# Sixteen batches of attention: the preparation stage moved between the units of the attention rows

## The chip, the cores and the metric

The program runs on one core of a Trainium2 chip, as one launch. The metric is the device time of that launch in microseconds (us). The engines named below are TensorE (PE: matmuls and transposes), VectorE (DVE), ScalarE (ACT), GpSimd (POOL) and SyncE (SP), whose queue issues every DMA of this program.

## The reference, cut to what matters

`x` is 16 batches of 512 positions by 128 features, float32. Attention has 16 heads of 8 features; a relative position, clipped to 20 on either side, adds a term to the scores and one to the output. The second half (a small attention, then a routed feed-forward layer with 9 experts) reads the same normalised input.

```python
xn = _layernorm(x)                                   # per position
q, k, v = proj(Wq, bq), proj(Wk, bk), proj(Wv, bv)   # of xn, 16 heads of 8
attn1 = einsum('bhqd,bhkd->bhqk', q, k)
attn2 = einsum('bhqd,qkd->bhqk', q, rel_k[idx])      # 41 relative places
attn = softmax((attn1 + attn2) / sqrt(8))
w1 = einsum('bhqk,bhkd->bhqd', attn, v)
w2 = einsum('bhqk,qkd->bhqd', attn, rel_v[idx])
x = x + (w1 + w2) @ Wo.T + bo + ffn(xn)
```

## The kernel before, in words

Four stages run one after the other, each with its own buffers and semaphores, and hand batches over through DRAM: `prepare`, `attend`, `mix`, `experts`. Positions stand on the 128 partitions, so a batch is four tiles of 128 by 128.

`prepare` goes over the 16 batches. For each it loads `X`, takes the statistics (L216, L227 on VectorE; L263, L266 on GpSimd), writes the normalised `XN`, transposes it on TensorE (L367) and copies it out as `XNT` (L327). Three projections follow: q (L352), k (L354), v (L357). Queries, keys and keys less the far-left term (`T[0]` to `T[2]`) are each split into three bf16 parts whose sum is the float32 value: a high part (L221, L316), the rest (L232, L273) cast to a middle part (L234, L323), and a low part (L248, L285). `QR` is the product of the queries with the 40 relative keys (L344, read out at L201 and L305). All of it goes to DRAM: `y` (x + bo), `xn`, nine `parts`, `v`, four tiles of `qr`, and `qr0`.

`attend` takes one batch as a row of 16 units. A unit u has four heads for each of the four blocks of 32 positions in a tile of 128 queries; it is worked in two pairs. In a pair, TensorE computes scores into one half of `b_s` (L682), VectorE adds the relative window (L815) and takes the maxima (L846), ScalarE exponentiates (L919), and in the next unit TensorE transposes the result (L694) into one of two PSUM banks, `b_pt`, from which ScalarE (L899) and VectorE (L832) copy it in turn. Three units later TensorE multiplies with v (L715). Everything that passes through the two banks is listed in `JOBS`; the banks alternate along that list, and a job waits until the reader of the job two places ahead is done (`bank_free`). Every fourth unit has "features" (L728, L732) for the relative output, read at L931 and L868, and multiplied in the next unit (L743). GpSimd makes windows (`make_window`), features and the `V` tiles (`make_v`).

Each engine's stream is written out by hand and keeps its order. SyncE issues, per row, windows in units 2, 6, 10 and 14 (`load_win`), features in units 1, 5, 9 and 13, the probabilities of each unit, and the 18 loads of the next row's queries and keys, spread over the units by the table `SPREAD` (`load_qk`, L566). The first scores of a row wait for all 18 (`qk_in`).

## Time and profile before

| | us |
|---|---|
| median of 3 runs | 2536.8 |
| lowest and highest | 2535.61, 2541.07 |
| the profiled execution | 2541.16 |
| its span in the profile | 2539.2 |

| engine | busy us | share of the span |
|---|---|---|
| PE | 2166.0 | 85% |
| DVE | 1971.7 | 78% |
| ACT | 1574.5 | 62% |
| POOL | 995.5 | 39% |

The profiled execution is one more run of the same program; its span is what the rows below add up to. The shares are means over four stages with different limits, so they don't say what bounds a stage. Stage 1 takes the first 234 us, attention 239 to about 1645 us, and the last two stages the rest.

### The profile page before, as it was taken

The page shows a single profiled execution, that of the slowest core. Times are in us where ns is not written, and L with a number is a line of the kernel's source. Part 1 is how long each engine was busy: PE and PEld are TensorE (multiplying, and loading weights), DVE is VectorE, ACT ScalarE, POOL GpSimd, SP SyncE. Part 2 cuts the span into 40 slices and gives each one's busy share as a digit, 9 for nine tenths or more (in the row PEclk, how much of TensorE's full clock was granted, in tenths as well). Part 3 has the DMA queues.
Part 4 walks back from the last instruction along what each step waited for, and adds up shares of the span by engine and source line. Part 5 has one row for each costly group of instructions (what it writes and reads, how often), then busy time and mean ns, then how long its engine had stood idle before and what let it go on. Part 6 is the DMA issues. An engine that isn't in the chain of part 4 may idle for free. (4 is left out here: it accounts for less than half of the span.)

```text
span 2539.2 us, 78048 instructions
## 1 busy us (share of the span) xinstructions
PE 2166.0 (85%) x27816; PEld 1483.5 (58%) x27816; DVE 1971.7 (78%) x4345; ACT 1574.5 (62%) x3954; POOL 995.5 (39%) x1318
## 2 busy tenths in 40 slices
PE   5673488888888888888888888789999996999999
PEld 3442366666666666666666666546666554666665
DVE  5664399898989889888999999646776765787777
ACT  4442378787877777777878787546777662232222
POOL 5664245445554555455545554300000003333332
PEclk9877699999999999999999999879999998999999
DMA  6887255555554555545555554300101011011010
GB/s 192 268 256 224 81 111 123 110 115 111 125 113 110 117 119 113 116 105 124 111 115 118 118 119 88 65 18 26 37 25 37 25 33 60 29 30 32 25 37 17
DMA packets 572137, 241.21 MB, mean 95 GB/s; under 512 B 466374, under 2 KB 535750, under 8 KB 567238
## 3 DMA queue, kind: packets, MB, share of 16 engines
q1 hardware_dynamic: 571846, 237.28, 37.5%
q8 instruction: 189, 3.10, 0.5%
q14 instruction: 102, 0.84, 0.1%
HBM read 133.87 MB, written 103.29 MB: 93 GB/s over the span
## 5 line engine op out<-in xcount | busy, mean ns | idle before, releaser
L919 ACT ACTIVATE a_probs<-a_bank_s,a_neg_max 128x512 f32<-128x512 f32 x1024 | 694.0, 684 | 203.2 <-DVE a_neg_max L846 199.6
L846 DVE TENSOR_REDUCE a_neg_max<-a_bank_s 128x2 f32<-128x1024 f32 x512 | 626.9, 1224 | 55.7 <-DVE a_bank_s L815 1.4
L694 PE MATMUL a_bank_pt<-a_ident,a_probs 128*128 128x128 f32 x4096 | 590.9, 284 | 54.2 <-ACT a_feat_t L931 42.3
L694 PEld LDWEIGHTS a_bank_pt<-a_ident,a_probs 128*128 128x128 f32 x4096 | 443.1, 142 | 193.1 <-issue 68.8
L899 ACT ACTIVATE a_probs_t<-a_bank_pt 128x512 f32<-128x512 f32 x512 | 304.9, 596 | 146.9 <-PE a_bank_pt L694 144.8
L832 DVE COPY a_probs_t<-a_bank_pt 128x512 f32<-128x512 f32 x512 | 349.3, 682 | 27.5 <-PE a_bank_pt L694 22.1
L715 PE MATMUL a_bank_o<-a_probs_t,a_v 128*32 128x128 f32 x8192 | 285.9, 282 | 1.0
L682 PE MATMUL a_bank_s<-a_kl,a_q 48*32 48x204 bf16 (+14 forms) x3840 | 156.2, 273 | 128.7 <-DMA a_kl<-scr_parts 78.9
L1589 ACT ACTIVATE e_gate<-e_bank_g 128x512 f32<-128x512 f32 x144 | 85.9, 597 | 275.8 <-PE e_bank_g L1528 275.8
L715 PEld LDWEIGHTS a_bank_o<-a_probs_t,a_v 128*32 128x32 f32 x8192 | 215.0, 112 | 56.7 <-issue 33.8
L1005 POOL TENSOR_TENSOR a_win<-a_raw,a_band 128x1152 f32<-128x1152 f32 x64 | 168.6, 2634 | 126.8 <-DVE a_neg_max L846 69.6
L815 DVE TENSOR_TENSOR a_bank_s<-a_bank_s,a_win 128x144 f32<-128x144 f32 (+2 forms) x640 | 161.4, 270 | 57.9 <-PE a_bank_s L682 52.7
L1536 PEld LDWEIGHTS e_bank_y<-e_w,e_hid 128*128 128x128 f32 x1152 | 149.5, 192 | 96.6 <-issue 57.0
L1278 DVE TENSOR_REDUCE m_neg_max<-m_bank_s 128x2 f32<-128x1024 f32 x128 | 156.6, 1224 | 61.4 <-PE m_bank_s L1242 54.1
L919 ACT ACTIVATION_READ_ACCUMULATOR a_probs<-a_bank_s,a_neg_max 128x1 f32 x1024 | 203.2, 198 | 0.0
L682 PEld LDWEIGHTS a_bank_s<-a_kl,a_q 48*32 48x32 bf16 x3840 | 63.2, 89 | 219.1 <-issue 203.6
L1375 ACT ACTIVATE m_probs<-m_bank_s,m_neg_max 128x512 f32<-128x512 f32 x256 | 173.3, 682 | 13.4 <-DVE m_neg_max L1278 5.0
L1251 PEld LDWEIGHTS m_bank_pt<-m_ident,m_probs 128*128 128x128 f32 x1024 | 112.5, 143 | 99.7 <-issue 83.4
L1536 PE MATMUL e_bank_y<-e_w,e_hid 128*128 128x128 f32 x1152 | 156.0, 279 | 17.1 <-DVE e_hid L1698 17.1
L682 PE MATMUL a_bank_s<-a_k,a_q 48*32 48x512 bf16 (+15 forms) x4096 | 169.3, 291 | 0.0
L1341 POOL TENSOR_TENSOR m_rms<-m_rms,m_pows 128x4 f32<-128x4 f32 x16 | 16.1, 1007 | 371.3 <-DVE m_rms L1291 371.3
L1613 DVE SCALAR_TENSOR_TENSOR e_y<-e_bank_y,e_comb,e_y 128x128 f32<-128x128 f32 x512 | 143.8, 343 | 12.3
(166 smaller groups left out, 3576.3 us busy)
## 6 DMA issues: line engine op xcount, KB each, us to landing
scr_probs<-a_probs SPq DMA_DIRECT2D x512, 72.0 KB, 2.7
a_raw<-scr_qr SPq DMA_DIRECT2D x256, 96.0 KB
scr_qr<-p_qr SPq DMA_DIRECT2D x64, 320.0 KB, 2.9
a_feat<-scr_probs SPq DMA_DIRECT2D x256, 78.0 KB, 2.4
scr_parts<-p_sp SPq DMA_DIRECT2D x144, 128.0 KB, 2.9
a_left<-scr_probs SPq DMA_DIRECT2D x256, 64.0 KB, 2.4
a_q<-scr_parts SPq DMA_DIRECT2D x32, 192.0 KB
a_k<-scr_parts SPq DMA_DIRECT2D x32, 192.0 KB
```

The costliest lines, as they stand in the source:

```text
L682: ins = nc.tensor.matmul(b_s[g * QBLK:(g + 1) * QBLK, p, a:z], Q[s][par:par + ROWS, half, at:at + QBLK], keys[s][par:par + ROWS, half, a:z ...
L694: ins = nc.tensor.transpose(b_pt[bank_of(job)][:, 0, t * P:(t + 1) * P], probs[(u - 1) % 4][:, j, MAX_REL + t * P:MAX_REL + (t + 1) * P], ...
L715: ins = nc.tensor.matmul(out, V[s][:, V_SLOTS.index((edge, kt)), j, hh * 24:hh * 24 + 32], blocks[:, :, :, kt * P + j * QBLK:kt * P + (j + ...
L815: ins = nc.vector.tensor_tensor(near, near, bass.AP(own.tensor, own.offset, [own.ap[0], [step, n], [1, z - a]]), ALU.add)
L832: nc.vector.tensor_copy(probs_t[(u - 1) // 2 % 2][:, spot(u - 1, PLACES[j]), :], b_pt[bank_of(job)][:, 0, :]).then_inc(pt_ev[bank_of(job)], 1)
L846: nc.vector.tensor_reduce(neg_max[:, 2 * pair:2 * pair + 2], b_s[:, 2 * pair:2 * pair + 2, :], AX.X, ALU.max, negate=True).then_inc(max_ok, 1)
L899: nc.scalar.activation(probs_t[(u - 1) // 2 % 2][:, spot(u - 1, PLACES[j]), :], b_pt[bank_of(job)][:, 0, :], ACT.Copy).then_inc(pt_ev[bank ...
L919: nc.scalar.activation(probs[u % 4][:, j, MAX_REL:MAX_REL + S], b_s[:, j, :], ACT.Exp, bias=neg_max[:, j:j + 1], accum_out=sums[:, t, PLAC ...
L1005: nc.gpsimd.tensor_tensor(win[t % 2][:], over, band[:].rearrange("p (o h c) -> p o h c", o=1, h=1) .to_broadcast([P, NQB, NJ, WIN]), ALU.m ...
L1278: nc.vector.tensor_reduce(neg_max[:, 2 * pair:2 * pair + 2], b_s[:, 2 * pair:2 * pair + 2, :], AX.X, ALU.max, negate=True).then_inc(max_ok, 1)
L1375: nc.scalar.activation(probs[:, j, :], b_s[:, j, :], ACT.Exp, bias=neg_max[:, j:j + 1], accum_out=sums[s][:, u, j:j + 1]).then_inc(exp_ok, 1)
L1536: ins = nc.tensor.matmul(b_y[k][:, t * P:(t + 1) * P], hid[k][:, t * P:(t + 1) * P], w2[:, e, :], start=True, stop=True)
```

## The change

`prepare` is gone; its buffers, now single instead of double, and its work are in `attend`. Row b, while it attends batch b, prepares batch b + 2 (`LEAD`). Twelve new jobs go through the two `b_pt` banks (`PREP`): the transposed input in unit 3, q in 5, k in 6, v in 13, and the relative products, two each in units 10, 11, 14 and 15. Batch 0 is prepared before any row (`prep(-LEAD, u)` on every engine), batch 1 in a row of its own (`lead=True`) beside the first loads. Rows 0 to 13 carry a preparation; rows 14 and 15 carry none.

Part by part:

- VectorE keeps the statistics (unit 0), `T[0]` (unit 5) and half of each relative read-out, to which a small copy into `QR0` is added. The normalising moves to GpSimd, as two passes over the whole tile; so does the rest and the low part of the queries.
- ScalarE makes `T[1]`, now `T[2]` from `T[1]`, all high and middle parts, `XNT`, and v directly into `v_in`: v no longer goes through DRAM.
- `y` is no longer stored. `attend` loads x again and GpSimd adds `bo` (`bo_ok`).
- A relative product contracts 64 rows of `T[0]` instead of 128.
- The 18 query and key loads now stand in units 3 to 14 instead of 0 to 14, since the low parts are stored in unit 1 of the same row and must have landed by unit 3.

```diff
...
 
-def prepare(nc, x, w, scr, ident_dram):
...
+LEAD = 2
 JOBS = [(u, "probs", j) for u in range(UNITS) for j in range(NJ)]
 JOBS += [(u, "features", n) for u in range(0, UNITS, 4) for n in range(2)] + [(9, "out", n) for n in range(2)]
+PREP = [(3, "xt", 0), (5, "q", 0), (6, "k", 0), (13, "v", 0)] + [(u, "qr", n) for u in (10, 11, 14, 15) for n in range(2)]
+JOBS += PREP
...
-        SPREAD = [1, 1, 2, 1, 1, 1, 2, 0, 1, 1, 2, 1, 2, 1, 1, 0]
+        SPREAD = [0, 0, 0, 2, 1, 1, 2, 2, 1, 1, 2, 1, 2, 2, 1, 0]
...
+            row(-1, 1, -1, lead=True)
...
 
-            def row(b, s, m, first=False, tail=False):
+            def prep(b, u):
+
+                n = b + LEAD
+                if n >= B:
+                    return
+                if u == 4:
+                    sp.wait_ge(xn_ok, n + 1)
+                    sp.dma_start(scr["xn"][n], X[:]).then_inc(out_xn, 16)
+                if u == 11:
+                    for k in range(3):
+                        sp.wait_ge(hi_ok[k], n + 1)
+                        sp.dma_start(scr["parts"][n, k, 0], SP[k][0][:]).then_inc(out_sp, 16)
+                if u == 12 and n + 1 < B:
+                    job_done(sp, b, (3, "xt", 0))
+                    sp.wait_ge(out_xn, 16 * n + 16)
+                    load_x(n + 1)
+                if u in (11, 12, 15):
+                    store_qr(b, (11, 12, 15).index(u))
+                if u == 15:
+                    for k in range(3):
+                        sp.wait_ge(mid_ok[k], n + 1)
+                        sp.dma_start(scr["parts"][n, k, 1], SP[k][1][:]).then_inc(out_sp, 16)
+
+            def store_qr(b, t):
+                n, u = b + LEAD, (10, 11, 14, 15)[t]
+                for hf in range(2):
+                    job_read(sp, b, (u, "qr", hf))
+                sp.dma_start(scr["qr"][n * NT + t], QR[t % 2][:].rearrange("p h r -> p (h r)")).then_inc(out_qr, 16)
+
+            def prep_rest(n):
+                store_qr(n - LEAD, NT - 1)
+                for i in range(NQB):
+                    rows_of = QR0[i * QBLK:(i + 1) * QBLK].rearrange("p t (g h) -> p (t g) h", h=NJ)
+                    sp.dma_start(scr["qr0"][n, :, :, i], rows_of).then_inc(out_0, 16)
+                for k in range(3):
+                    sp.wait_ge(lo_ok[k], n + 1)
+                    sp.dma_start(scr["parts"][n, k, 2], SP[k][2][:]).then_inc(out_sp, 16)
+
+            def row(b, s, m, first=False, tail=False, lead=False):
                 last = isinstance(b, int) and b == B - 1
                 for u in range(12 if tail else UNITS):
                     t = u // 4
...
 
                     if not tail and u % 4 == 2 and not (last and t >= NT - 2):
+                        if t == 1 and not last:
+                            sp.wait_ge(out_qr, 16 * NT * (b + 2))
                         load_win(b + (t >= NT - 2), (t + 2) % NT)
                     if u % 4 == 1 and not (first if u == 1 else tail):
                         read_features(b, u)
-                    if not tail and not last and u == 0:
+                    if not tail and not last and u == 1:
+                        prep_rest(b + 1)
+                    if not tail and not last and u == 3:
+                        need(sp, s_ps, b, 2 * UNITS, 0)
...
+            for u in range(UNITS):
+                prep(-LEAD, u)
+            prep_rest(0)
...
+            def prep(b, u):
+                n = b + LEAD
+                if n >= B:
+                    return
+                for job in PREP:
+                    if job[0] != u:
+                        continue
+                    bank = b_pt[bank_of(job)][:, 0]
+                    bank_free(pe, b, job)
+                    if job[1] == "xt":
+                        pe.wait_ge(xn_ok, n + 1)
+                        for t in range(NT):
+                            ins = nc.tensor.transpose(bank[:, t * P:(t + 1) * P], X[:, t, :], ident[:])
+                    elif job[1] in ("q", "k"):
+                        job_read(pe, b, (3, "xt", 0))
+                        ins = nc.tensor.matmul(bank, (wq if job[1] == "q" else wk)[:], XNT[:], start=True, stop=True)
+                    elif job[1] == "v":
+                        for t in range(NT):
+                            ins = nc.tensor.matmul(bank[:, t * P:(t + 1) * P], XNT[:, t * P:(t + 1) * P], wv[:],
+                                                   start=True, stop=True)
+                    else:
+                        job_read(pe, b, (5, "q", 0))
+                        t, hf = (10, 11, 14, 15).index(u), job[2]
+                        rows_of = slice(hf * HALF, hf * HALF + HALF)
+                        ins = nc.tensor.matmul(bank[:, 0:G * FAR], T[0][rows_of, t * P:(t + 1) * P],
+                                               relx[rows_of, hf::2, :], start=True, stop=True)
+                    ins.then_inc(pt_ps, 1)
 
             def scores(b, u, pair, s):
...
-
+                    prep(b, u)
+
+            for u in range(UNITS):
...
+            def read_qr(b, u, t):
+                n, job = b + LEAD, (u, "qr", 0)
+                bank = b_pt[bank_of(job)][:, 0, 0:G * FAR].rearrange("p (h r) -> p h r", r=FAR)
+                job_done(v, b, job)
+                need(v, out_qr, n, 16 * NT, 16 * 2 * (t // 2))
+                need(v, out_0, n, 16 * NQB, 0)
+                nc.vector.tensor_copy(QR0[:, t, 0::2], bank[:, :, 0])
+                nc.vector.tensor_copy(QR[t % 2][:, 0::2, :], bank).then_inc(pt_ev[bank_of(job)], 1)
+
+            def prep(b, u):
+                n = b + LEAD
+                if n >= B:
+                    return
+                if u == 0:
+                    v.wait_ge(x_in, 16 * n + 16)
+                    need(v, xn_ok, n, 1, 0)
+                    for t in range(NT):
+                        ins = nc.vector.bn_stats(stats[:, t, :], X[:, t, :])
+                    ins.then_inc(stats_ok, 1)
+                    v.wait_ge(stats_ok, n + 1)
+                    for t in range(NT):
+                        ins = nc.vector.bn_aggr(mv[:, t, :], stats[:, t, :])
+                    ins.then_inc(mv_ok, 1)
+                if u == 5:
+                    job = (5, "q", 0)
+                    job_done(v, b, job)
+                    need(v, rest_ok[0], n, 1, 0)
+                    v.wait_ge(prep_ok, 3)
+                    nc.vector.tensor_scalar(T[0][:], b_pt[bank_of(job)][:, 0, :], Q_SCALE, bias_q[:], ALU.mult, ALU.add
...
+            def read_qr(b, u, t):
+                n, job = b + LEAD, (u, "qr", 1)
+                bank = b_pt[bank_of(job)][:, 0, 0:G * FAR].rearrange("p (h r) -> p h r", r=FAR)
+                job_done(act, b, job)
+                need(act, out_qr, n, 16 * NT, 16 * 2 * (t // 2))
+                need(act, out_0, n, 16 * NQB, 0)
+                nc.scalar.activation(QR0[:, t, 1::2], bank[:, :, 0], ACT.Copy)
+                nc.scalar.activation(QR[t % 2][:, 1::2, :], bank, ACT.Copy).then_inc(pt_ev[bank_of(job)], 1)
+
+            def high(n, k):
+                need(act, out_sp, n, PART_STORES, 0)
+                nc.scalar.activation(SP[k][0][:], T[k][:], ACT.Copy).then_inc(hi_ok[k], 1)
+
+            def middle(n, k):
+                act.wait_ge(rest_ok[k], n + 1)
+                nc.scalar.activation(SP[k][1][:], rest[k][:], ACT.Copy).then_inc(mid_ok[k], 1)
+
+            def prep(b, u):
+                n = b + LEAD
+                if n >= B:
+                    return
...
+                    job = (3, "xt", 0)
+                    job_done(act, b, job)
+                    nc.scalar.activation(XNT[:], b_pt[bank_of(job)][:, 0, :], ACT.Copy).then_inc(pt_ev[bank_of(job)], 1)
...
+                    job = (6, "k", 0)
+                    job_done(act, b, job)
+                    need(act, lo_ok[1], n, 1, 0)
+                    nc.scalar.activation(T[1][:], b_pt[bank_of(job)][:, 0, :], ACT.Identity, bias=qk_bias[:, 1:2]
+                                         ).then_inc(pt_ev[bank_of(job)], 1)
+                    job_read(act, b, (5, "q", 0))
+                    high(n, 0)
+                if u == 7:
+                    job_read(act, b, (6, "k", 0))
+                    high(n, 1)
+                    need(act, lo_ok[2], n, 1, 0)
+                    nc.scalar.activation(T[2][:], T[1][:], ACT.Identity, bias=left_less[:]).then_inc(t2_ok, 1)
+                if u == 9:
+                    act.wait_ge(t2_ok, n + 1)
+                    high(n, 2)
+                if u in (10, 11, 14, 15):
+                    read_qr(b, u, (10, 11, 14, 15).index(u))
+                if u in (12, 13, 14):
+                    middle(n, u - 12)
...
+                        act.wait_ge(const_ok, N_CONST_OK - 1)
+                    nc.scalar.activation(v_in[:], b_pt[bank_of(job)][:, 0, :].rearrange("p (t e) -> p t e", e=E), ACT.Copy
+                                         ).then_inc(pt_ev[bank_of(job)], 1)
+
...
+            def prep(b, step):
+                n = b + LEAD
+                if n >= B:
+                    return
+                if step == 0:
+                    g.wait_ge(mv_ok, n + 1)
+                    nc.gpsimd.tensor_tensor(rstd[:], mv[:, :, 1], pows[:, 0:1].to_broadcast([P, NT]), ALU.add
+                                            ).then_inc(rstd_add, 1)
+                    g.wait_ge(rstd_add, n + 1)
+                    nc.gpsimd.tensor_tensor(rstd[:], rstd[:], pows[:, 1:2].to_broadcast([P, NT]), ALU.pow).then_inc(rstd_ok, 1)
+                    nc.gpsimd.tensor_tensor(X[:], X[:], mv[:, :, 0:1].to_broadcast([P, NT, E]), ALU.subtract
+                                            ).then_inc(x_less, 1)
+                    g.wait_ge(rstd_ok, n + 1)
+                    g.wait_ge(x_less, n + 1)
+                    nc.gpsimd.tensor_tensor(X[:], X[:], rstd[:].rearrange("p (t o) -> p t o", o=1).to_broadcast([P, NT, E]),
+                                            ALU.mult).then_inc(xn_ok, 1)
+                if step == 2:
+                    g.wait_ge(t2_ok, n + 1)
+                    for k in range(3):
+                        g.wait_ge(hi_ok[k], n + 1)
+                        need(g, lo_ok[k], n, 1, 0)
+                        nc.gpsimd.tensor_tensor(rest[k][:], T[k][:], SP[k][0][:], ALU.subtract).then_inc(rest_ok[k], 1)
+                if step == 3:
+                    need(g, out_sp, n, PART_STORES, 0)
+                    for k in range(3):
+                        g.wait_ge(mid_ok[k], n + 1)
+                        nc.gpsimd.tensor_tensor(SP[k][2][:], rest[k][:], SP[k][1][:], ALU.subtract).then_inc(lo_ok[k], 1)
+
...
                         scale(b)
+                    if t == 0:
+                        prep(b, 0)
...
-                        make_v(b + 1, t, 1 - s)
+                    if not last and t < 2:
+                        for kt in (2 * t, 2 * t + 1):
+                            make_v(b + 1, kt, 1 - s)
                     if t == 2 and not first:
                         add_out(b)
+                    if t > 1:
+                        prep(b, t)
 
             def scale(b):
...
-    prepare(nc, a["x"], a, scr, a["ident"])
...
```

TensorE at the end of unit 10 and the start of unit 11 of a row, before. L715 is the product with v, L694 the transposes of the probabilities, L682 the scores:

```order
L715 MATMUL a_bank_o<-a_probs_t,a_v 32x128 x16
L694 MATMUL a_bank_pt<-a_ident,a_probs 128x128 x8
L682 MATMUL a_bank_s<-a_kl,a_q 32x236 x4
L682 MATMUL a_bank_s<-a_kl,a_q 32x300 x4
L682 MATMUL a_bank_s<-a_k,a_q 32x276 x4
L682 MATMUL a_bank_s<-a_k,a_q 32x212 x4
L694 MATMUL a_bank_pt<-a_ident,a_probs 128x128 x8
```

The same place now (L500, L479 and L467 are the same operations):

```order
L500 MATMUL a_bank_o<-a_probs_t,a_v 32x128 x16
L479 MATMUL a_bank_pt<-a_ident,a_probs 128x128 x8
L449 MATMUL a_bank_pt<-a_relx,a_t 128x320 x2
L467 MATMUL a_bank_s<-a_kl,a_q 32x236 x4
L467 MATMUL a_bank_s<-a_kl,a_q 32x300 x4
L467 MATMUL a_bank_s<-a_k,a_q 32x276 x4
L467 MATMUL a_bank_s<-a_k,a_q 32x212 x4
L479 MATMUL a_bank_pt<-a_ident,a_probs 128x128 x8
```

Two products of 320 columns stand between the last transposes of a unit and the scores of the next.

VectorE at the end of unit 11, before. L846 is the maxima, L832 the copy of a transposed tile, L825 sums of moved probabilities, L815 the window of unit 12:

```order
L846 TENSOR_REDUCE a_neg_max<-a_bank_s 128x2
L832 COPY a_probs_t<-a_bank_pt 128x512
L825 TENSOR_REDUCE a_moved<-a_probs 128x2 x4
L815 TENSOR_TENSOR a_bank_s<-a_bank_s,a_win 128x2x72
L846 TENSOR_REDUCE a_neg_max<-a_bank_s 128x2
```

The same place now (L688, L670, L663 and L653 are the same operations, L597 and L598 read the relative product out):

```order
L688 TENSOR_REDUCE a_neg_max<-a_bank_s 128x2
L670 COPY a_probs_t<-a_bank_pt 128x512
L663 TENSOR_REDUCE a_moved<-a_probs 128x2 x4
L597 COPY a_qr_first<-a_bank_pt 128x8
L598 COPY a_qr<-a_bank_pt 128x8x40
L653 TENSOR_TENSOR a_bank_s<-a_bank_s,a_win 128x2x72
L688 TENSOR_REDUCE a_neg_max<-a_bank_s 128x2
```

The two copies out of the relative product stand behind the sums and ahead of the next window.

SyncE in units 11 to 13, before. L566 loads keys, L632 stores the output, L643 stores probabilities, L600 and L606 load features:

```order
L643 DMA scr_probs<-a_probs 128x2x72 x2
L566 DMA a_kl<-scr_parts 16x1x4096
L632 DMA scr_y<-a_y_in 128x512
L643 DMA scr_probs<-a_probs 128x2x72 x2
L566 DMA a_kl<-scr_parts 8x4096
L566 DMA a_kl<-scr_parts 24x1x4096
L643 DMA scr_probs<-a_probs 128x2x72 x2
L600 DMA a_left<-scr_probs 32x16x32 x4
```

Now (L272 loads keys, L323 stores high parts, L339 a relative tile, L250 loads the x of a later batch, L391 stores probabilities, L302 loads features):

```order
L391 DMA scr_probs<-a_probs 128x2x72 x2
L323 DMA scr_parts<-a_sp 128x512 x3
L339 DMA scr_qr<-a_qr 128x640
L272 DMA a_kl<-scr_parts 24x1x4096
L380 DMA scr_y<-a_y_in 128x512
L391 DMA scr_probs<-a_probs 128x2x72 x2
L250 DMA a_x<-in_x 128x4x128
L339 DMA scr_qr<-a_qr 128x640
L272 DMA a_kl<-scr_parts 16x1x4096
L272 DMA a_kl<-scr_parts 8x4096
L391 DMA scr_probs<-a_probs 128x2x72 x2
L302 DMA a_left<-scr_probs 32x16x32 x4
```

Six DMAs of the preparation stand in these two units, ahead of the key loads of units 11 and 12.

## Rows read from the trace of the kernel before

**Rows 1.** Windows of the trace: us, each engine's busy us, TensorE's clock, DMA share, GB/s.

```profile
10.00:234.00 224.00, 147.32 (x512) 95.26 (x512) 142.44 (x336) 102.23 (x193) 144.48 (x224) 0.85 0.83 252
234.00:284.30 50.30, 0.00 (x0) 0.00 (x0) 4.74 (x14) 0.00 (x0) 6.68 (x5) 0.50 0.29 86
384.20:1630.20 1246.00, 1089.45 (x19844) 799.86 (x19844) 1117.94 (x2259) 975.70 (x2463) 619.10 (x911) 0.98 0.50 113
```

**Rows 2.** Timeline, first batch in stage 1: start, us, engine, line, tiles, count.

```profile
9.91 0.86 DVE L216 BATCH_NORM_STATS2 p_stats<-p_x 128x6 f32<-128x128 f32 x4
...
32.58 2.79 SPq L169 DMA_DIRECT2D scr_qr<-p_qr  x4
```

**Rows 3.** Timeline, start of the attention stage.

```profile
243.49 2.59 SPq L574 DMA_DIRECT2D a_left_of<-scr_qr  x4
...
248.53 4.00 SPq L566 DMA_DIRECT2D a_q<-scr_parts  x6
...
284.35 0.23 PE L682 MATMUL a_bank_s<-a_kl,a_q 48*32 48x44 bf16 x4 [60.70 <-DMA a_kl<-scr_parts]
```

**Rows 4.** Waits in 384.2 to 1630.2: us in total, times, longest.

```profile
ACT a_probs_t L899 <- PE a_bank_pt L694: 132.7, 194, 2.4
...
ACT a_probs L919 <- DVE a_neg_max L846: 128.1, 294, 0.9
...
DVE a_last_t L868 <- PE a_bank_pt L732: 25.3, 60, 0.4
...
PE a_bank_s L682 <- DMA a_kl<-scr_parts: 17.1, 10, 2.4
DVE a_probs_t L832 <- PE a_bank_pt L694: 15.9, 20, 1.9
DVE a_bank_s L815 <- PE a_bank_s L682: 14.3, 26, 1.9
```

**Rows 5.** Timeline of TensorE, end of unit 3 of a row.

```profile
644.00 0.63 PE L728 MATMUL a_bank_pt<-a_ident,a_feat 128*128 128x128 f32 x4 [0.66 <-ACT a_probs_t L899]
...
644.95 0.27 PE L682 MATMUL a_bank_s<-a_kl,a_q 48*32 48x108 bf16 x8
```

**Rows 6.** Timeline of VectorE, the same place and the next row's start.

```profile
645.06 0.29 DVE L868 COPY a_last_t<-a_bank_pt 128x128 f32<-128x128 f32 x1 [0.42 <-PE a_bank_pt L732]
...
703.11 0.36 DVE L815 TENSOR_TENSOR a_bank_s<-a_bank_s,a_win 128x52 f32<-128x52 f32 x2 [1.02 <-PE a_bank_s L682]
```

**Rows 7.** Timeline of ScalarE in a unit without features.

```profile
662.50 0.69 ACT L919 ACTIVATE a_probs<-a_bank_s,a_neg_max 128x512 f32<-128x512 f32 x1 [0.78 <-DVE a_neg_max L846]
```

**Rows 8.** Timeline, a later batch in stage 1.

```profile
42.43 1.02 PE L352 MATMUL p_bank_q<-p_xnt,p_wq 128*128 128x512 f32 x2
...
44.16 0.86 DVE L216 BATCH_NORM_STATS2 p_stats<-p_x 128x6 f32<-128x128 f32 x4
...
45.04 2.32 PE L344 MATMUL p_bank_qr<-p_relx,p_t 128*128 128x320 f32 x8
```

**Rows 9.** Groups by line: busy us, mean ns of one, idle before.

```profile
L285 POOL TENSOR_TENSOR p_sp<-p_rest,p_sp 128x512 bf16<-128x512 f32 x32 | 43.3, 1370 | 0.1
...
L201 DVE COPY p_qr<-p_bank_qr 128x320 f32<-128x320 f32 x64 | 31.2, 487 | 43.2 <-PE p_bank_qr L344 41.3 <-DMA scr_qr<-p_qr 1.8
...
L1045 POOL TENSOR_TENSOR a_o_sb<-a_o_sb,a_moved_t 128x512 f32<-128x512 f32 x16 | 20.4, 1273 | 103.1 <-DVE a_o_sb L876 103.1
...
L323 ACT ACTIVATE p_sp<-p_rest 128x512 bf16<-128x512 f32 x32 | 20.2, 632 | 21.4 <-POOL p_rest L273 21.4
...
L211 DVE TENSOR_SCALAR p_t<-p_bank_q,p_bias_q 128x512 f32<-128x512 f32 x16 | 12.0, 750 | 13.0 <-PE p_bank_q L352 13.0
```

**Rows 10.** SyncE: the last key load (timeline); its longest wait (waits, 384.2 to 1630.2).

```profile
698.00 0.33 SPq L566 DMA_DIRECT2D a_kl<-scr_parts  x1
...
SPq L643 <- ACT a_probs L919: 294.6, 149, 4.9
```

**Rows 11.** Window in which only the query and key loads still run.

```profile
270.00:275.00 5.00, 0.00 (x0) 0.00 (x0) 0.00 (x0) 0.00 (x0) 0.00 (x0) 0.50 0.13 54
```

431 lines of the change are left out of this document (120 added, 311 removed).

## The prediction

> **What bounds the kernel now.** I read the stages first, since the page's shares are means over four of them. The windows [rows 1] show stage 1 moving 252 GB/s with its DMA engines 83% busy for 224 us, and then 50 us in which nothing computes: the hand-over. Attention from the second row to the end is 1246 us for 15 rows, 83.07 us each, with VectorE busy for 1117.9. The waits of that stretch [rows 4] then say which engine has room. ScalarE waits 132.7 + 128.1 us there, 17.4 per row, for TensorE or VectorE. VectorE's three largest waits make 25.3 + 15.9 + 14.3 = 55.5 us, 3.7 per row; what else separates 1118 from 1246 is small gaps between dependent instructions. So in attention each row lasts as long as VectorE's list, and an edit is worth what it adds to that list or makes it wait. Last I followed single units in the timelines [rows 5 to 7]: in unit 4, which has extra jobs in the two banks, TensorE waits 0.66 us for ScalarE to free a bank, VectorE then waits 0.42 us for the new result, and the next scores start 0.95 us after the first extra job.
>
> **What is removed.** Before, the first scores start at 284.35 us [rows 3]. Now a first batch must still pass every step before them. In stage 1 the first batch took from 9.91 to 32.58 + 2.79 = 35.4, so 25.5 us [rows 2]. Now its statistics stand behind attention's constants on VectorE, which were 4.74 busy us in the hand-over [rows 1]; I take 4; two whole-tile passes on GpSimd at 1.27 us each [rows 9] replace a pass spread over four tiles, and nothing of it overlaps another batch: some 3 us; the last stores must land: 3 us. So 9.9 + 4 + 25.5 + 3 + 3 = 45 us. From the first load of attention's data to the first scores took 284.35 - 243.49 = 40.9 us [rows 3], and that stays: 86 us. Batch 1 is prepared meanwhile, but its stores stand on SyncE behind the 18 loads, two relative buffers wait for them, and TensorE's row 0 stands behind its last product: 6 us more. First scores at 92 us instead of 284.35: 192 us gained. From both sides: 80 us if the loads of batch 0 go faster and batch 1 costs nothing, 105 if batch 1's stores are late by as much again.
>
> **What is added, per row, to VectorE.** All 14 rows 0 to 13 pay it.
>
> - Statistics, unit 0: 0.86 us for four tiles [rows 8]; the aggregation has no row here, lies between 0 and that, and I take 0.5 with the wait between. 1.35 us. Nothing covers it.
> - `T[0]`, unit 5: 0.75 us [rows 9]. It needs q, 1.02 us on TensorE [rows 8], which stands behind the product with the feature weights. VectorE has a sum and a reciprocal to do meanwhile and then waits; I take 0.65, between nothing and q's whole 1.02. 1.4 us.
> - Relative read-outs, units 10, 11, 14, 15: 0.49 us each [rows 9], plus a copy of 128 by 8, which no row shows; the bounds are 0 and 0.49, and I take 0.15, since it has a fortieth of the elements and mostly a fixed cost. 2.55 us. The two products of a unit take 2.32 / 4 = 0.58 us each [rows 8]. The first hides behind VectorE's copy of the last transposed tile. The second needs the bank that this copy frees, and the next scores stand behind it: 0.5 us of waiting in units 10 and 14; in 11 and 15 the sums of moved probabilities cover it. 3.6 us in all. With no cover anywhere it would be 4.6.
> - xt, k and v, which ScalarE reads: only their time on TensorE matters to VectorE, through the scores behind them. TensorE is ahead of VectorE by about 0.7 us at a unit's end (VectorE's wait of 0.42 [rows 6] against 0.66 + 0.63 of TensorE's [rows 5]). xt 0.1, k (1.02) 0.3; v stands in unit 13 behind the feature weights, 0.9. 1.3 us; nothing if TensorE had 1 us more of lead, 2.7 if none.
> - ScalarE: ten more passes over a whole tile at 0.63 us [rows 9] and four relative read-outs, taken like VectorE's at 0.64: 8.9 us of its 17.4 us of idle time. It idles 0.78 us ahead of the exponentials between units 7 and 8 [rows 7]. Units 6 and 7 add two passes, 1.3 us, so these come 0.5 us late, and the scores behind them have about that much slack. 0.5 us per row. If its idle time were gone, each of the ten passes would show in full.
> - Start of a row: VectorE waited 1.02 us at 703.11 [rows 6], behind TensorE's wait for key loads, 17.1 us in 10 rows [rows 4]. The last load is issued at 698.00 [rows 10]. Now one more load stands in unit 13 and 0.7 us more of issue, but units 13 to 15 are longer by 2.7 us. I take 0.3 us, and 0.5 for what I have not seen.
> - GpSimd: nine passes (six for the splits, two to normalise, one for `bo`) at 1.27 to 1.37 us [rows 9] and two small ones, 13 us per row, on 619.1 / 15 = 41.3 us [rows 1] of 83. The windows are made in the same order, and v no longer comes over DRAM. Nothing. If it were late, the features of a unit would be, and VectorE behind them.
> - SyncE: 19 more DMAs and one less, at 0.33 us [rows 10] to 0.67 (4.00 / 6) [rows 3]: 6 to 12 us per row. It waits 294.6 / 15 = 19.6 us per row for exponentials [rows 10], which hides them. Behind it stand only its own loads; those that TensorE waits for were costed above, at the start of a row.
>
> Sum: 1.35 + 1.4 + 3.6 + 1.3 + 0.5 + 0.8 = 8.95, say 9.0 us; 4.6 of it is VectorE's own work and 4.4 waiting. Fourteen rows: 126 us. A row becomes 92 us.
>
> **The sum.** 2539.2 - 192 + 126 = 2473 us of span. The profiled execution's own time is 2.0 above its span, and 4.4 above the median of the runs shown, so the median comes out at 2473 + 2.0 - 4.4 = 2471 us, 2.6% less. Mix and experts are not touched.
>
> **The rivals.**
>
> *Slower: the two banks pass no overlap on.* Twelve jobs join a ring of two banks. If every job added its TensorE time (0.63 for xt like the features, 3 x 1.02, 4 x 1.16: 8.3 us) and the bank's hand-over where a new reader is involved (0.66 [rows 5], eight groups, 5.3 us), and VectorE did only its statistics outside that, a row would grow by 8.3 + 5.3 + 1.35 = 15 us: 14 x 15 = 210, median 2555. It decides from 192 / 14 = 13.7 us a row. For it: the extra jobs of unit 4 cost TensorE exactly this. Against it: VectorE felt only 0.42 of it.
>
> *The key loads come late.* From the first query load at 248.53 to the scores at 284.35, 35.8 us [rows 3], one batch's loads move, and towards the end only 0.13 of 16 DMA engines work, at 54 GB/s [rows 11]: two engines carry the tail. In a row these two have 36 us of loads, and their part of the rest, about 0.44 of 83 us or 37 us (0.50 [rows 1] less these loads). The change brings 0.83 x 224 / 16 = 11.6 us per batch [rows 1] less the dropped v and y, say 9. That is 82 of 92 us; but the loads now stand in 12 units of 69 us, where it is 36 + 30 + 6 = 72. So the last may be 3 us late, each row: 42 us more, median 2513. Only from 4.7 us a row would the change lose. The Trainium skill, "DMA: Bandwidth & Descriptors", section "Why a DMA increments its semaphore by 16 and not by 1", says that a transfer is spread over the largest number up to 16 that divides the outermost sizes of both its sides. By that rule the loads with three and two slots outermost run on three and two engines, and the two busiest get 816 of 2304 KB. By that rule, the trace agrees: two engines' share at the tail.
>
> *All waits are absorbed.* If VectorE's present 3.7 us of waits take up the new ones, a row grows by 4.6 us: 64 us, median 2409. Against it: the new jobs come in other units than the present waits.
>
> *No difference.* A row grows by 13.7 us, from a mixture of these.
>
> **How the numbers follow.** My forecast 50%, key loads late 20%, all absorbed 10%, no overlap 15%, no difference 5%. The predicted time is the likeliest case's. The first scores can be 12 us earlier or 13 later, and the open terms of a row sum to 7 or 11.5: 2430 to 2520. The late loads reach 2513 and more, the no-difference case 2532; below 2430 and above 2535 I leave out the absorbed case and the slower one, together some 2 in 10. A difference under 0.2%, 5 us, is about what a measurement of this kernel can't tell. Faster: 0.50 + 0.20 + 0.10 = 0.80; same 0.05; slower 0.15.
>
> **What would show it.** The first scores of a row 0 at about 92 us. Rows at a distance of 92 us in the first 14, and of 83 in the last two. VectorE's waits per row up by some 4 us, most of it ahead of `T[0]`, and ahead of windows in units 11, 14 and 15. ScalarE busier by nearly 9 us per row and still waiting. TensorE's wait for key loads at a row's start near 1 us: at 4 it is the second rival. Rows of 97 us and more would make the prediction wrong, and so would first scores after 110 us; a wait of VectorE or TensorE for GpSimd, or of SyncE for a store, is the one that I have priced at nothing.

## The result, and the profile after

The changed kernel took 2528.4 us, median of 20 runs (2516.0 to 2540.4), beside 2539.6 us for the kernel before (2533.2 to 2545.3) in runs on the same chip. The ratio is 0.995, with a 95% interval from 0.9937 to 0.9964: 0.5% less, clear of the scatter between runs. The forecast was 2471 us, 2.6% less. The profiled execution has a span of 2530.6 us where the one before had 2539.2.

The first lines of the page after:

```profile
span 2530.6 us, 77225 instructions
...
PE 2189.7 (87%) x27816; PEld 1471.0 (58%) x27816; DVE 1898.9 (75%) x4279; ACT 1591.1 (63%) x4050; POOL 1030.8 (41%) x1270
```

The timeline of TensorE holds the first term of the forecast, the first scores, which stood at 284.35 us before [rows 3]:

```profile
94.56 0.23 PE L467 MATMUL a_bank_s<-a_kl,a_q 48*32 48x44 bf16 x4
```

They start at 94.56 us, so 189.8 us are gained there; the forecast had 192. All that is missing must be in the rows. For these I take ScalarE's copy of `o_sb`, once per row: before it stood at 384.2 for the first and 1630.2 for the last batch, now (the view of its source line: duration min, median, max, then first and last start):

```profile
L831 ACT ACTIVATE a_o_sb<-a_bank_o x16: 591/593/597, 204.2 to 1621.1; 128x512 f32<-128x512 f32 x16
```

That splits the whole span. From the first scores to the first copy: 109.6 us, before 99.9, so 9.8 more. From the first to the last copy, 15 rows, of which 13 prepare another batch: 1416.9 us, before 1246.0, so 170.9 more. After the last copy: 909.5 and 909.0. Sum: -189.8 + 9.8 + 170.9 + 0.5 = -8.6 us, the difference of the spans. Over the 14 rows that prepare, 180.7 us would be 12.9 each, where the forecast had 9.0. They are not all there, though: the last two distances between copies, which hold no preparation, are 95.8 and 74.1 us where they were 83.3 and 72.6, so 14.0 us more. That leaves 166.7 us, 11.9 for each of the 14. TensorE's longest wait for key loads stands at the end of row 14:

```profile
1528.70 0.23 PE L467 MATMUL a_bank_s<-a_kl,a_q 48*32 48x44 bf16 x4 [11.63 <-DMA a_kl<-scr_parts]
```

The window of these 15 rows, after, and below it the waits in it (us in total, times, longest), which answer to [rows 1] and [rows 4] (the window's numbers are us, the busy time of PE, PEld, DVE, ACT and POOL, then TensorE's granted clock, DMA share and GB/s):

```profile
204.20:1621.10 1416.90, 1219.69 (x20260) 863.29 (x20260) 1173.70 (x2472) 1070.40 (x2698) 764.07 (x1052) 0.96 0.52 125
```

```profile
ACT a_probs_t L799 <- PE a_bank_pt L479: 207.5, 231, 11.6
...
ACT a_probs L825 <- DVE a_neg_max L688: 130.8, 267, 1.6
DVE a_bank_s L653 <- PE a_bank_s L467: 111.7, 94, 11.1
POOL a_left L924 <- DMA a_left<-scr_probs: 87.7, 27, 7.3
PE a_bank_s L467 <- DMA a_kl<-scr_parts: 62.3, 14, 11.6
```

VectorE is busy 55.8 us longer than before, 4.3 us for each of the 13 rows; the forecast had 4.6 of its own work. But its wait for TensorE's scores went from 14.3 to 111.7 us, and TensorE's for key loads from 17.1 us in 10 rows to 62.3 in 14, 4.45 us each. The forecast had named that number: at 4 it is the second rival. SyncE's own waits show a companion, the stores of probabilities. It awaits their landing before it reads features, and its own loads stand behind that wait. Of the same view of before, over its 15 rows, the second row read 38.1 us in 21 waits:

```profile
SPq L391 <- ACT a_probs L825: 228.9, 106, 9.7
SPq L296 <- DMA scr_probs<-a_probs: 81.6, 34, 6.2
```

The timeline around one such row start. The last three key loads are issued at 757.24 and 761.99; TensorE ended the old row's relative products at 760.43 and stands until 768.17, and VectorE with it:

```profile
757.24 1.42 SPq L272 DMA_DIRECT2D a_kl<-scr_parts  x2
758.70 1.24 SPq L391 DMA_DIRECT2D scr_probs<-a_probs  x2
758.80 1.63 PE L449 MATMUL a_bank_pt<-a_relx,a_t 64*128 64x320 f32 x4 [0.35 <-ACT a_probs_t L799]
...
760.07 1.88 SPq L290 DMA_DIRECT2D a_raw<-scr_qr  x4
761.99 0.35 SPq L272 DMA_DIRECT2D a_kl<-scr_parts  x1
...
768.17 0.22 PE L467 MATMUL a_bank_s<-a_kl,a_q 48*32 48x44 bf16 x4 [7.74 <-DMA a_kl<-scr_parts]
...
769.03 0.36 DVE L653 TENSOR_TENSOR a_bank_s<-a_bank_s,a_win 128x52 f32<-128x52 f32 x2 [8.44 <-PE a_bank_s L467]
```

Over rows 2 to 12 the last load is issued 1.8 us before TensorE is through with the old row (before: 3.1), and the scores start 6.0 us after its issue (before: 4.5). So it is issued later, and what the scores wait for lands later too.

The stall also costs something after it has ended. TensorE's granted clock fell while it stood, from 1.00 to 0.50 (2.4 to 1.2 GHz), and eight transposes behind the restart take 1.97 us where they took 1.09:

```profile
754.00:760.00 6.00, 5.63 (x86) 3.59 (x86) 5.15 (x13) 5.19 (x15) 2.84 (x5) 1.00 0.55 96
770.00:772.00 2.00, 2.00 (x36) 1.20 (x38) 1.88 (x4) 1.72 (x4) 1.84 (x3) 0.50 0.03 6
```

```profile
757.36 1.09 PE L479 MATMUL a_bank_pt<-a_ident,a_probs 128*128 128x128 f32 x8
...
768.73 1.97 PE L479 MATMUL a_bank_pt<-a_ident,a_probs 128*128 128x128 f32 x8
```

Unit by unit, as the distance of VectorE's first maxima in successive units, mean of rows 2 to 12, the growth over the kernel before sits in a few places (us):

```
unit         0     1    3    5    6    7     9    10   11   13   14    15    sum
after     +2.21 -0.42 +.36 +.71 +.31 +.07 +.08 +1.37 +.96 +.61 +1.37 +4.45  +12.1
```

Unit 15, whose distance ends with the next row's first maximum, holds the wait, and unit 0 holds, beside the statistics, the restart at the lower clock. So two questions are left: why the loads are late, and whether the rest is what the forecast said.

### The profile page after: what moved, and what is told of

The parts are those of the page before. It is cut to its first block and busy times, and to the rows that moved or that the text cites. A ratio compares the mean times of both kernels' runs of the same rounds, so it can differ in the third digit from the quotient of the medians.

```text
span 2530.6 us, 77225 instructions
## 1 busy us (share of the span) xinstructions
PE 2189.7 (87%) x27816; PEld 1471.0 (58%) x27816; DVE 1898.9 (75%) x4279; ACT 1591.1 (63%) x4050; POOL 1030.8 (41%) x1270
## 5 line engine op out<-in xcount | busy, mean ns | idle before, releaser
L825 ACT ACTIVATE a_probs<-a_bank_s,a_neg_max 128x512 f32<-128x512 f32 x1024 | 694.0, 684 | 145.6 <-DVE a_neg_max L688 143.8
L688 DVE TENSOR_REDUCE a_neg_max<-a_bank_s 128x2 f32<-128x1024 f32 x512 | 627.0, 1225 | 55.4 <-DVE a_bank_s L653 1.8
L479 PE MATMUL a_bank_pt<-a_ident,a_probs 128*128 128x128 f32 x4096 | 598.8, 288 | 57.5 <-ACT a_feat_t L837 40.6
L479 PEld LDWEIGHTS a_bank_pt<-a_ident,a_probs 128*128 128x128 f32 x4096 | 453.2, 145 | 192.8 <-issue 79.8
L670 DVE COPY a_probs_t<-a_bank_pt 128x512 f32<-128x512 f32 x512 | 349.8, 683 | 37.4 <-PE a_bank_pt L479 33.0
L500 PE MATMUL a_bank_o<-a_probs_t,a_v 128*32 128x128 f32 x8192 | 290.9, 285 | 1.3
L500 PEld LDWEIGHTS a_bank_o<-a_probs_t,a_v 128*32 128x32 f32 x8192 | 219.1, 114 | 60.3 <-issue 39.7
L653 DVE TENSOR_TENSOR a_bank_s<-a_bank_s,a_win 128x144 f32<-128x144 f32 (+2 forms) x640 | 161.6, 272 | 119.0 <-PE a_bank_s L467 116.1
L467 PE MATMUL a_bank_s<-a_kl,a_q 48*32 48x204 bf16 (+14 forms) x3840 | 155.9, 274 | 82.2 <-DMA a_kl<-scr_parts 62.3
L1491 PEld LDWEIGHTS e_bank_y<-e_w,e_hid 128*128 128x128 f32 x1152 | 149.4, 192 | 95.7 <-issue 56.7
L825 ACT ACTIVATION_READ_ACCUMULATOR a_probs<-a_bank_s,a_neg_max 128x1 f32 x1024 | 203.7, 199 | 0.0
L467 PEld LDWEIGHTS a_bank_s<-a_kl,a_q 48*32 48x32 bf16 x3840 | 59.6, 89 | 202.4 <-issue 188.7
L467 PE MATMUL a_bank_s<-a_k,a_q 48*32 48x512 bf16 (+15 forms) x4096 | 170.5, 298 | 0.0
L449 PE MATMUL a_bank_pt<-a_relx,a_t 64*128 64x320 f32 x256 | 106.5, 515 | 61.6 <-DVE a_qr L598 32.6
```

Source lines behind the costliest of these rows:

```text
L467: ins = nc.tensor.matmul(b_s[g * QBLK:(g + 1) * QBLK, p, a:z], Q[s][par:par + ROWS, half, at:at + QBLK], keys[s][par:par + ROWS, half, a:z ...
L479: ins = nc.tensor.transpose(b_pt[bank_of(job)][:, 0, t * P:(t + 1) * P], probs[(u - 1) % 4][:, j, MAX_REL + t * P:MAX_REL + (t + 1) * P], ...
L500: ins = nc.tensor.matmul(out, V[s][:, V_SLOTS.index((edge, kt)), j, hh * 24:hh * 24 + 32], blocks[:, :, :, kt * P + j * QBLK:kt * P + (j + ...
L653: ins = nc.vector.tensor_tensor(near, near, bass.AP(own.tensor, own.offset, [own.ap[0], [step, n], [1, z - a]]), ALU.add)
L670: nc.vector.tensor_copy(probs_t[(u - 1) // 2 % 2][:, spot(u - 1, PLACES[j]), :], b_pt[bank_of(job)][:, 0, :]).then_inc(pt_ev[bank_of(job)], 1)
L688: nc.vector.tensor_reduce(neg_max[:, 2 * pair:2 * pair + 2], b_s[:, 2 * pair:2 * pair + 2, :], AX.X, ALU.max, negate=True).then_inc(max_ok, 1)
```

## The experiments

All ratios are to the kernel before, in runs on the same chip (its median there lay between 2536.8 and 2547 us). "Row" is the mean distance of the `o_sb` copies in each profiled execution, over 15 rows.

| kernel | us, median | ratio (95%) | first scores | row |
|---|---|---|---|---|
| before | 2539.6 | | 284.4 | 83.1 |
| changed | 2528.4 | 0.995 (0.9937 to 0.9964) | 94.6 | 94.5 |
| before, new table | 2620.7 | 1.030 (1.028 to 1.032) | 281.6 | 88.1 |
| before, one-slot loads | 2509.9 | 0.986 (0.983 to 0.989) | 274.8 | 82.3 |
| changed, one-slot loads | 2450.0 | 0.962 (0.959 to 0.966) | 90.8 | 89.4 |
| changed, loads from unit 0 | 2465.2 | 0.969 (0.967 to 0.972) | 95.7 | 89.7 |
| changed, large loads first | 2491.1 | 0.981 (0.977 to 0.985) | 96.5 | 91.3 |
| changed, thin stores | 2501.7 | 0.984 (0.980 to 0.988) | 94.7 | 92.2 |
| one-slot, from unit 0 | 2442.1 | 0.961 (0.957 to 0.965) | 78.0 | 89.5 |
| one-slot, read-outs on ScalarE | 2435.2 | 0.958 (0.954 to 0.962) | 83.0 | 88.9 |
| one-slot, short relative products | 2427.2 | 0.955 (0.952 to 0.959) | 75.6 | 88.5 |
| one-slot, from unit 0, ScalarE | 2427.7 | 0.955 (0.952 to 0.957) | 80.9 | 88.9 |
| changed, margins first | 2526.0 | 0.996 (0.993 to 0.998) | 94.0 | 93.7 |
| one-slot, from unit 0, ScalarE, margins first | 2430.3 | 0.959 (0.956 to 0.962) | 78.6 | 88.9 |

**The table of loads alone, in the kernel before.** The change had to begin the loads of the next row in unit 3, since their parts are not stored earlier, and the table `SPREAD` packs them closer toward the end.

```diff
-        SPREAD = [1, 1, 2, 1, 1, 1, 2, 0, 1, 1, 2, 1, 2, 1, 1, 0]
+        SPREAD = [0, 0, 0, 2, 1, 1, 2, 2, 1, 1, 2, 1, 2, 2, 1, 0]
```

> The kernel before, with nothing of the change but its table of loads: none in units 0 to 2, two in units 3, 6, 7, 9 to 14 where the table says so, the last in unit 14. Theory A (the key loads confined to a few DMA engines in fewer units come late by themselves): the wait of TensorE for key loads and of SyncE for the stores of exponentials grows here too, by 2 to 4 us a row, 30 to 60 us over the kernel, ratio 1.012 to 1.024. Theory B (the preparation's own 19 DMAs a row make the traffic that delays them): the table costs under 0.5 us a row here, ratio 1.000 to 1.003. Theory C (SyncE has too much to issue): as B, no cost here.

It is 3.0% slower, more than theory A had asked for: a row takes 5.0 us more, with nothing prepared in it. Its window of 15 rows and its wait for key loads:

```profile
387.40:1708.40 1321.00, 1120.29 (x19844) 820.75 (x19844) 1120.93 (x2259) 976.17 (x2464) 620.06 (x911) 0.95 0.47 106
```

```profile
PE a_bank_s L682 <- DMA a_kl<-scr_parts: 69.8, 14, 6.5
```

VectorE has 1121 us of work, 1118 in [rows 1], and TensorE's wait is 69.8 us in place of 17.1. The table alone has the fault of the changed kernel. Theories B and C fall as its only cause.

**The loads cut into slots, in both kernels.** Same bytes, same places in the table, but each load is one head slot of 8 partitions by 8 KB, 36 loads for 18.

```diff
-        STACK = [(n, par, group) for n in range(3) for par in range(2) for group in range(PARTS)]
-        SPREAD = [0, 0, 0, 2, 1, 1, 2, 2, 1, 1, 2, 1, 2, 2, 1, 0]
+        STACK = [(n, par, slot) for n in range(3) for par in range(2) for slot in range(SLOTS)]
+        SPREAD = [2 * k for k in (0, 0, 0, 2, 1, 1, 2, 2, 1, 1, 2, 1, 2, 2, 1, 0)]
...
-                    slots = [slot for slot in range(SLOTS) if Q_PART[slot] == group]
-                    part, step = (group, 0) if n == 0 else (0, P * S)
+                    slots, step = [group], 0
+                    part = Q_PART[group] if n == 0 else K_PART[group]
```

> The changed kernel with each load cut into loads of one head slot, 36 of 64 KB in place of 18 of up to 192 KB, so that the outermost size is 8 rows and not 2 or 3. Theory A: the load is spread over eight DMA engines, the backlog of the two busiest goes, TensorE's wait for key loads falls from 62 us to under 20 and SyncE's for exponentials' stores from 83 to about 30; gain 3 to 4 us a row, 2470 to 2485 us, ratio 0.973 to 0.980. Theory B: no change in the bytes, ratio 0.990 to 0.997. Theory C: 18 DMAs more for SyncE per row, slower than the changed kernel, ratio 0.997 to 1.005.

> The kernel before with the same loads of one head slot, as a control: its key loads cost it 17 us of TensorE's waiting in attention, and the 36 us ahead of the first scores become shorter. Theory A: at most 1 to 2 us a row and some 10 us at attention's start better, 2505 to 2530 us, ratio 0.987 to 0.997; the gap between this and the changed kernel with the same loads is then that of the forecast, 50 to 70 us. Theory B: no difference, ratio 0.998 to 1.002. Theory C: slower by the issue of 18 more DMAs, up to 1.005.

Both as theory A expected, the changed kernel by more than its range, the control in its range of time (2505 to 2530 us); the two lie 59.9 us apart, where 50 to 70 was expected. The changed kernel gains 4.9 us a row (96.2 to 91.2 in rows 2 to 12): 4.5 in unit 15 and 1.6 in unit 0, less 1.0 in units 1 and 9, where the one-slot run has the 1.2 GHz clock in some rows (unit 1 then takes 5.82 us, else 5.00; unit 9 8.0, else 6.51). The control gains 1.15 us a row (84.1 to 82.9), since the kernel before had some lateness of its own. What the change added by late loads is thus 3.8 us a row. In row 14, without a preparation, the changed kernel took 12.1 us more than the one before; the two one-slot kernels differ there by 0.25. TensorE's wait for key loads is 1.7 us, once, and SyncE's for stores of probabilities 1.6 us. Twice as many DMAs on SyncE cost nothing that shows, so theory C has nothing for it. Whether the loads really ran on few engines is read where nothing else runs, ahead of the first scores. The control, in windows (DMA share and GB/s last):

```profile
256.00:260.00 4.00, 0.00 (x0) 0.00 (x0) 0.00 (x0) 0.00 (x0) 0.00 (x0) 0.50 0.53 96
260.00:264.00 4.00, 0.00 (x0) 0.00 (x0) 0.00 (x0) 0.00 (x0) 0.00 (x0) 0.50 0.75 115
264.00:268.00 4.00, 0.00 (x0) 0.00 (x0) 0.00 (x0) 0.00 (x0) 0.00 (x0) 0.50 0.49 90
268.00:272.00 4.00, 0.00 (x0) 0.00 (x0) 0.00 (x0) 0.00 (x0) 0.00 (x0) 0.50 0.54 98
```

The second stretch also holds a load of v and two stores, issued from 259.41 us. In the others the share is 0.49 to 0.54 of 16 engines, as of eight busy ones, where it was 0.13, as of two, with the old loads [rows 11]. The same in the changed kernel, whose loads have the old form:

```profile
70.00:75.00 5.00, 0.00 (x0) 0.00 (x0) 0.00 (x0) 0.00 (x0) 0.00 (x0) 0.50 0.12 52
75.00:80.00 5.00, 0.00 (x0) 0.00 (x0) 0.00 (x0) 0.00 (x0) 0.00 (x0) 0.50 0.13 56
```

The Trainium skill, "DMA: Bandwidth & Descriptors", section "Why a DMA increments its semaphore by 16 and not by 1", has a transfer spread over the largest number up to 16 that divides both outermost sizes. By that rule a load of 8 rows runs on eight engines and one of two slots on two; the trace agrees, 0.49 to 0.54 and 0.12 to 0.13.

**The old loads, from unit 0 again.** The changed kernel with the table of before; six query loads come first, whose parts are stored by then.

```diff
-        SPREAD = [0, 0, 0, 2, 1, 1, 2, 2, 1, 1, 2, 1, 2, 2, 1, 0]
+        STACK = [(0, par, group) for par in range(2) for group in range(2)] + [(0, 0, 2), (0, 1, 2)]
+        STACK += [(n, par, group) for n in (1, 2) for par in range(2) for group in range(PARTS)]
+        SPREAD = [1, 1, 2, 1, 1, 1, 2, 0, 1, 1, 2, 1, 2, 1, 1, 0]
...
-                    if not tail and not last and u == 3:
+                    if not tail and not last and u == 0:
                         need(sp, s_ps, b, 2 * UNITS, 0)
+                        sp.wait_ge(out_sp, PART_STORES * (b + 1) + 16 * 6)
+                    if not tail and not last and u == 3:
                         sp.wait_ge(out_sp, PART_STORES * (b + 2))
```

> The changed kernel with loads spread as before over units 0 to 14: six query loads, whose parts are stored by then, in units 0 to 2. Theory A: the two busiest DMA engines get back 15 us of time per row, unit 15 with the row's start shrinks from 10.4 us toward 6, gain 2 to 4 us a row, 2470 to 2500 us, ratio to before 0.973 to 0.985. Theory B or C: the same number of DMAs and bytes, so within 1 us a row of the changed kernel, ratio 0.990 to 0.997.

It gives back 4.85 us a row (91.3), more than theory A's range and as much as the slots do: unit 15 grows by 0.20 us in place of 4.45. Two quite different cures reach the same row.

**Large loads first, and thin stores.** Two ways to ask what makes the last loads late. The first changes only the order.

```diff
-        STACK = [(n, par, group) for n in range(3) for par in range(2) for group in range(PARTS)]
+        STACK = [(n, par, group) for group in range(PARTS) for n in range(3) for par in range(2)]
```

> The changed kernel, same table and same 18 loads, but in the order three-slot loads first, then the two-slot, then the one-slot ones, so that the last four units issue 64 and 128 KB loads that are spread over more DMA engines or are short. Theory A1 (the last loads are late because the busiest DMA engines still have the row's large loads ahead of them at its end): TensorE's wait for key loads falls from 62 us to under 30, gain 1.5 to 3 us a row, ratio 0.978 to 0.987. Theory A2 (over the row as a whole the two busiest engines have more than a row's time of work): the order changes nothing, ratio 0.993 to 0.998.

A row gets 3.3 us shorter in rows 2 to 12, and the wait for key loads falls from 62.3 to 26.5 us: A1, with a rest of 1.7 us a row over the one-slot run. The last load is issued no earlier than before (1.4 us ahead of TensorE's end, 1.8 without the edit), but the scores follow 3.0 us after it and not 6.0. So it is mostly the backlog at the end of a row, less the sum over a row.

The second leaves the preparation's traffic out: 8 columns of each store from batch 2 on, with as many DMAs, and loads that read batch `b % 2`; the output of the later batches is left out by that.

```diff
+                        w_ = S if n < LEAD else 8
-                        sp.dma_start(scr["parts"][n, k, 0], SP[k][0][:]).then_inc(out_sp, 16)
+                        sp.dma_start(scr["parts"][n, k, 0][:, 0:w_], SP[k][0][:, 0:w_]).then_inc(out_sp, 16)
```

> The changed kernel in which the stores of the split parts, of the normalised input and of the relative products of batches 2 to 15 are only 8 columns wide, with as many DMAs; the loads read the parts of batch 0 or 1, so the output of the later batches is left out. Theory A (the loads' own place and shape make them late, as in the kernel before with the new table, which lost 5.0 us a row without any of these stores): a part comes back at most, 0 to 2 us a row, ratio 0.985 to 0.997. Theory B (the stores' 2.4 MB per row are the cause): the whole 4.9 us a row comes back, ratio 0.965 to 0.972.

2.4 us of the 4.9 come back in rows 2 to 12, 1.1% in the ratio: a part, just past what A allowed and half of what B asked. Here the last load is issued 4.6 us ahead of TensorE's end, and the scores still follow 6.3 us after it: what comes back is SyncE's time. The stores of the change make the lateness worse, but the table alone brings it.

**Both cures together.** The one-slot loads, spread from unit 0 (the two diffs above, joined).

> The changed kernel with both cures at once: 36 one-slot loads, and spread over units 0 to 14. One cause, cured by either: the cures don't add up, within 0.3% of the run with one-slot loads alone, ratio 0.958 to 0.966. Two causes: another 1 to 2 us a row, ratio 0.950 to 0.957.

The row is the same, 89.5 against 89.4 us: one cause, cured by either. The median is 8 us lower, no more than the 12.7 us by which the first scores came earlier in this profile.

**What the rest of a row costs.** With the loads out of the way, the forecast's terms can be read: the one-slot changed kernel against the one-slot kernel before.

```
unit                          0    1    3    5    6    7    9    10    11    13    14    15   sum
changed less before, us    +1.01 -.02 +.37 +.97 +.31 +.08 +.49 +1.37 +1.06 +.90 +1.38 +.39  +8.3
```

The sum is 8.3 us where the forecast had 9.0. Some figures are not all work: unit 0 costs 1.16 us between rows that both have the 2.4 GHz clock (6.61 and 5.45), unit 9 nothing (6.51 and 6.50), and unit 15 0.97 between rows that don't wait for loads (5.92 and 4.95), since the control still waits for its own in most rows. Two runs ask what paces units 10 to 15. In one ScalarE makes every relative read-out; its `read_qr`:

```diff
-                n, job = b + LEAD, (u, "qr", 1)
+                n = b + LEAD
+                for hf in range(2):
+                    job = (u, "qr", hf)
...
-                if u in (10, 11, 14, 15):
-                    read_qr(b, u, (10, 11, 14, 15).index(u))
```

The last two lines are VectorE's call.

> The one-slot loads, and every relative read-out on ScalarE, so that VectorE's list is shorter by four read-outs, 4 x (0.49 + 0.17) = 2.6 us a row, and ScalarE's longer by as much. If a row is as long as VectorE's list and TensorE's second product waits for one bank either way: gain 1.5 to 2.6 us a row, ratio 0.949 to 0.955. If in these units TensorE and the banks set the pace, because ScalarE now reads both banks one after the other: within 1 us a row of the one-slot run either way, ratio 0.957 to 0.968.

VectorE is busy 28.3 us less in its 13 rows, 2.2 each, but units 10, 11 and 14 still grow by 1.33, 1.22 and 1.37 us, and the row shrinks by 0.7 us, in units 1 and 9, where the clock now stays at 2.4 GHz in all rows but one. So VectorE's own 0.65 us is not what these units pay. In the other the products are cut to 40 of 320 columns, which leaves the relative products of seven heads in eight out.

```diff
-                        ins = nc.tensor.matmul(bank[:, 0:G * FAR], T[0][rows_of, t * P:(t + 1) * P],
-                                               relx[rows_of, hf::2, :], start=True, stop=True)
+                        heads = G if n < LEAD else 1
+                        ins = nc.tensor.matmul(bank[:, 0:heads * FAR], T[0][rows_of, t * P:(t + 1) * P],
+                                               relx[rows_of, hf:2 * heads:2, :], start=True, stop=True)
```

> The run with one-slot loads, in which the relative products of batches 2 to 15 are made for one head in eight only (40 columns in place of 320); the read-outs stay as long as they were, and the other heads' products are left out of the output. Theory P (the two products, 1.58 us together on TensorE, set the pace of units 10, 11 and 14): these three units give back 1 to 1.3 us each, 3 to 4 us a row, ratio 0.938 to 0.945. Theory V (the forecast's: VectorE's own read-out of 0.65 us in each of four units, and half a microsecond of waiting in two of them): 0.5 us each in units 10 and 14, 1 us a row, ratio 0.955 to 0.959.

Units 10 and 14 give back 0.35 and 0.40 us, unit 15 0.27, and unit 11 takes 0.26 more. P is refuted. Theory V had priced 0.5 each in units 10 and 14, so it is near; that the whole row is 1.15 us shorter, as V said, is luck, since 0.86 of that lies in units 1 and 9, by the clock, and 0.38 is lost in unit 0, by the clock too. The ratio of 0.955 owes more to first scores 15 us earlier in the profile. What stays when either is shortened are the hand-overs: in the one-slot run TensorE waits for ScalarE to free one bank, then its weight load for VectorE to free the other, and then VectorE waits for the scores behind both.

```profile
1057.99 1.58 PE L449 MATMUL a_bank_pt<-a_relx,a_t 64*128 64x320 f32 x4 [0.55 <-ACT a_probs_t L799]
1058.04 0.68 DVE L670 COPY a_probs_t<-a_bank_pt 128x512 f32<-128x512 f32 x1
...
1058.77 0.29 PEld L449 LDWEIGHTS a_bank_pt<-a_relx,a_t 64*128 64x128 f32 x2 [0.49 <-DVE a_probs_t L670]
...
1058.91 0.48 DVE L598 COPY a_qr<-a_bank_pt 128x320 f32<-128x320 f32 x1
...
1059.99 0.32 DVE L653 TENSOR_TENSOR a_bank_s<-a_bank_s,a_win 128x144 f32<-128x144 f32 x1 [0.59 <-PE a_bank_s L467]
```

That the hand-overs set the pace is argued from these rows and the two runs; no run takes them away.

**The version that beats both.** One-slot loads from unit 0, read-outs on ScalarE.

> One-slot loads, spread over units 0 to 14, relative read-outs on ScalarE: the candidate to beat both kernels. The run with one-slot loads and ScalarE's read-outs had 0.9584, the spread on top of one-slot loads took off 0.002. If they add up: 0.955 to 0.960, 2425 to 2440 us. If the spread brings nothing here, 0.958 to 0.962.

2427.7 us, ratio 0.955 (0.952 to 0.957): 4.5% under the kernel before. The interval overlaps those of the two runs that it joins, so that their gains add up is not shown.

**The margins first.** In the changed kernel SyncE stands 19.4 us between its first loads and batch 1's stores, for a store of one number, the last of three small ones that fill margins in DRAM. Two runs issue that store and two small ones ahead of the loads.

```diff
+            sp.wait_ge(const_ok, N_CONST_OK)
+            for at in PROBS_AT:
...
+            sp.dma_start(scr["qr"][B * NT, 0:1, 0:1], ident[0:1, 0:1]).then_inc(margin_out, 16)
             load_left(0, 0)
             load_win(0, 0)
             load_qk(0, 0, STACK)
```

> The changed kernel, with the three small stores (two of 64 numbers, one of a single number) that SyncE issues behind the first 18 loads and whose landing it waits 19.4 us for issued ahead of those loads. Theory M (that wait sets the first scores, through batch 1's stores behind it): the wait goes, first scores near 76 us in place of 94.6, 15 to 19 us off the whole, ratio 0.988 to 0.991. Rival N (the loads themselves, 36 us of them, set the first scores): first scores stay at 90 us or more, ratio 0.994 to 0.997.

> The best so far (one-slot loads, spread over units 0 to 14, relative read-outs on ScalarE) with the same three stores ahead of the first loads. There the wait was 6.4 us and the first scores at 81 us. Theory M: 5 to 6 us less, ratio 0.950 to 0.954. Rival N: unchanged, ratio 0.953 to 0.957.

The wait is gone and the time is not: first scores at 94.03 us, ratio 0.996, so theory M falls and N holds. With the best version nothing is gained in the ratio either: 0.959 and 0.955, intervals that overlap, and above the range of both theories. Only its profile shows first scores 2.3 us earlier. SyncE's timeline in the first of the two runs shows where it stands now; the same three stores of parts took it 1.39 us to issue in the changed kernel:

```profile
65.04 7.50 SPq L290 DMA_DIRECT2D a_raw<-scr_qr  x4
72.58 2.22 SPq L319 DMA_DIRECT2D scr_xn<-a_x  x1
74.85 8.12 SPq L323 DMA_DIRECT2D scr_parts<-a_sp  x3
```

## Why the forecast was right in its direction and wrong in its size

- **What bounds the kernel** was read rightly: VectorE's list, to which the change adds 4.3 us a row (forecast 4.6). Its small terms came close: the wait ahead of `T[0]` is 8.8 us in 13 rows, 0.68 each (0.65); the copy of 128 by 8 takes 0.16 us (0.15).

```profile
L619 DVE TENSOR_SCALAR a_t<-a_bank_pt,a_bias_q 128x512 f32<-128x512 f32 x13 | 9.8, 751 | 8.8 <-PE a_bank_pt L440 8.8
```

- **What is removed**, 192 us, measured 189.8. Its 6 us for batch 1 had the right place: from SyncE's first issue behind the loads, at 84.34 us, to the first scores take 10.2. What holds the start before that are the 18 loads, for half of their 36 us with a DMA share of 0.17 or less.
- **What is added, without the loads**, 9.0 us less the 0.8 for the row's start and the unseen: statistics 1.0 (1.35), `T[0]` 0.97 (1.4), relative read-outs 4.2 (3.6), xt, k and v 1.6 (1.3), ScalarE 0.1 (0.5), and 0.5 in unit 9, by the clock, for which there was no term; the sum of all units is 8.3. The relative read-outs came near their price for the wrong reason: units 11 and 15 were to be covered by the sums of moved probabilities, and unit 11 costs 1.06 us, unit 15 0.97 where the control doesn't wait.
- **The step that failed is "Start of a row: ... I take 0.3 us".** It asked only how much later the last load is issued, and set against that 2.7 us of longer units. Measured, late loads add 3.8 us a row over the kernel before (12.1 in rows 2 to 12, less the 8.3 between the one-slot kernels), and 12.1 us in row 14, which was to stay at 83; either cure takes 4.9 us from the changed kernel. The price depends on how the loads before the last one drain: on few engines, closer together toward the end, behind stores that SyncE must await. That last wait, priced at nothing, went from 38.1 to 81.6 us. The forecast also had no term for TensorE's clock, which is at 1.2 GHz behind each stall. That two engines carry a backlog within a row is argued from the runs; no row numbers the engines. The rival "The key loads come late" said much of this and had 20%; its 3 us a row were too low, and it had nothing for row 14. Its 816 of 2304 KB are the part of each of the two busiest engines. The table alone costs 5.0 us a row in a kernel without any preparation, and had the forecast priced the table by itself, as one edit, it would have seen a part of the change that can only lose.
- **The sum**: 57.6 us above the forecast's span, of which 54.7 in the rows (180.7 for 126) and 2.6 in the first scores. Of the 54.7, 14.0 lie in the last two distances and 40.7 in the 14 rows with a preparation, 11.9 us each for 9.0. In rows 2 to 12, with 12.1, the gap of 3.1 is late loads, 3.8 for 0.3, less 0.35 by which the other terms were too dear (8.3 for 8.65). With late loads at 3 us the rival gave 2513; measured 2528.
- **The other rivals** did not come: GpSimd's extra work cost nothing that shows (TensorE's weight loads wait for its features once a row, 15.3 us in all, and units 4, 8 and 12 don't grow), nor did the issue of SyncE's extra DMAs; with all terms but late loads a row grows by 8.3 us and not 15, and the waits were not absorbed. "No difference" asked for 192 us from a mixture; with 180.7 the size came near it, mostly from terms that had been priced and one that failed.
- **First scores in the other runs**: in five of the six changed kernels with one-slot loads they follow SyncE's wait for the store of one number: waits of 2.6, 4.3, 6.4, 9.0 and 17.8 us go with first scores at 75.6, 78.0, 80.9, 83.0 and 90.8 us. The sixth has that store ahead of the loads and 78.6. In the five kernels with the old loads the scores start between 94.0 and 96.5 us, with a wait of 19.3 to 19.5 us or without it.
- **Not settled**: why that store, behind the same one-slot loads, lands after 2.6 us in one run and after 17.8 in another; and why the loads come latest, 11.6 us, in row 14, which has the least to do.

## What to carry to other kernels

When work is merged into a loop, price the schedule of what was already there: a table of loads that must start later is an edit of its own, and it can cost more than the added arithmetic. Look also at the rows that the change leaves alone: row 14, without any added work, was 12.1 us longer. Count DMA load by engine, not as a mean: a share of 0.50 over a row says nothing on the two engines that one kind of load runs on. Look at the outermost size of a transfer's shape before its bytes; 36 loads of 64 KB beat 18 larger ones by 3.3% here, at no cost in issue that shows.

## What was not expected of the hardware

- Two DMA engines, by their share, moved 52 to 56 GB/s alone, some 27 each; eight moved 90 to 98, some 12 each. With loads of eight rows the engines are faster together and slower each: over the rows the DMA share rose from 0.50 to 0.56 in the kernel before at 113 and 114 GB/s, and the time fell. No run says what holds each engine back.
- A stall of TensorE is paid twice. Unit 0 takes 6.61 us in the one-slot changed kernel and 7.6 to 8.8 behind the stalls of the changed one, in each of rows 2 to 12, with the granted clock at 1.2 GHz around the restart.
- SyncE's issue of a DMA is not a constant: the same three stores took it 1.39 us and, behind an undrained backlog, 8.12. A wait removed there came back as issue time.
- A store of one number took 19.4 us to land behind the loads, and 2.6 to 17.8 us with one-slot loads. The Trainium skill's same page and section puts a transfer of one element on one engine, and a transfer on fewer than 16 on the lowest-numbered ones, so that it would stand behind every load; no row here numbers the engines.
